# End of a routing stage: the last top two moved ahead of the one-hots, twenty one-hots on GpSimd, and the first low expert weights made before the block ends

## The chip, the cores and the metric

The kernel runs on one core of one Trainium2 chip. A core has five engines that run side by side and meet at semaphores: PE (TensorE, matrix multiply), DVE (VectorE), ACT (ScalarE), POOL (GpSimd) and SP (SyncE, which here only issues DMAs). The metric is the device time in microseconds (us) of one execution, the median over several runs.

## The reference, cut to what matters

Rows `x` of 4 x 1024 tokens with 256 features go through attention with 16 heads, a layer norm, a mixture of experts, and a second layer norm.

```
x = layernorm(x + attention(x))                      # 4096 tokens, 256 features
probs = softmax(x @ gate_W)                          # 8 experts
topk_w, topk_idx = top_k(probs, 2); topk_w /= topk_w.sum(-1)
out = 0.5 * gelu(x @ shared_W + shared_b)
for e in range(8):
    h = gelu(x @ W1[e] + b1[e])                      # 256 -> 1024
    out += combine[:, e] * (h @ W2[e] + b2[e])       # 1024 -> 256
x = layernorm(x + out) * gamma + beta
```

## The kernel before, in words

The program has three stages, each a block of its own: `attention`, `tokens`, `experts` (the second layer norm is the end of the third). A block ends when all five engines have come to its end; only then does the next one begin on any of them.

The change is all in `tokens`, with one line in `experts`. `tokens` goes over 32 tiles of 128 tokens. For each it projects the attention's output (PE, L1052), adds and normalises (DVE, ACT), turns the rows (PE, L1061), multiplies them with the shared and gate weights (PE, L1069), and adds the bias (DVE, L1262). The tiles are routed in four parts: tiles 0 to 7, 8 to 15, 16 to 27 (the third part, `LAST - 1` in the code) and 28 to 31 (the last, `LAST`). For a part there follow:

- `top` (DVE, L1272 to L1285): the two best experts of each token, twelve small instructions each waiting for the one before.
- `rank` (PE, L1077 and L1078; for the last part `last_rank`, L1084 and L1086): how many tokens before this one chose the same expert. For the third part it waits for a running count that POOL makes (L992, L994).
- `places` (DVE, L1293 to L1299): splits a token's place in its expert's list into a high part and a low part of 128.
- `lows`: for each tile and each of the two choices one instruction of 128 x 128 that writes the low part as a one-hot, `low_hot`, 16 bit. Parts one and two have them on POOL (L1002, 16 each), the third on DVE (L1307, 24) and the last on DVE (L1307, 8).

When the last part's counts are there (`totals`, L1096 and L1098), DVE works out where each expert's list begins (L1367 to L1379), and makes the high one-hots in five pieces (`ones_at`, L1313); ACT multiplies each by the row's number (L1202). PE then multiplies low one-hots with high ones (`sort`, L1105, 64 matmuls into one bank): the result says which token stands in each place of the experts' chunks. The five calls of `sort` take choice one of tiles 0 to 15, choice two of tiles 0 to 15, choice one of tiles 16 to 31, choice two of tiles 16 to 23, and choice two of tiles 24 to 31. DVE turns the result into row numbers (L1405 to L1417), POOL gathers the first chunk's rows with two indirect DMAs (L1037), and the block ends. In between DVE makes a small plan of experts (L1384 to L1390); when it is there, SP loads the first expert's weights `up` and `down`.

Matrix products in `experts` are made of three: high times high, low times high, high times low. So each weight is split by ACT into a rounded high part and by DVE into the rest, the low part. The first expert's `up_h` is made by ACT at the end of `tokens` (L1205); its `up_l` by DVE as its first work in `experts` (line L1822, which a helper shares with `e_xl`, the low part of the chunk's turned rows, and `e_w2l`, that of the down weights). PE's first matmuls of `experts` (L1744) need `e_xl`.

Every engine's order is the order in which the code was written; there is no scheduler.

## Time and profile before

| | us |
|---|---|
| median of 3 runs | 1809.6 (1808.56 to 1811.19) |
| the profiled execution | 1826.84 |
| its span, first instruction to last | 1825.1 |
| PE busy | 1730.8 (95%) |
| DVE busy | 1373.6 (75%) |
| ACT busy | 1025.7 (56%) |
| POOL busy | 380.3 (21%) |

The shares are means over the whole program. `attention` ends and `tokens` begins near 1151 us of the span, and `experts` begins at 1338.9 us; the stretch in which the changed code stands is about 1300 to 1342 us, and there no engine is busy all the time. Times in the rows are microseconds from the start of the span unless they are marked ns.

### The profile page before, as it was taken

What the parts mean: (1) busy time and instruction counts of PE and PEld (TensorE: products, weight loads), DVE (VectorE), ACT (ScalarE), POOL (GpSimd) and SP (SyncE); (2) the same over time, 40 slices, a digit from 0 to 9 for tenths busy, and PEclk for the clock granted to TensorE, in tenths of its full rate; (3) what the DMA queues carried; (4) which work ended last, traced back from release to release, by engine and by line L of the source; (5) the groups of instructions that cost most, each with busy time, mean ns of one, the idle gap of its engine ahead of it and who ended that gap; (6) DMA issues with size and microseconds to landing.
All of it is one profiled execution on the core that took longest, in us unless ns stands there. A gap on an engine that the chain in (4) does not pass through costs nothing. (4 is left out here: it accounts for less than half of the span.)

```text
span 1825.1 us, 31876 instructions
## 1 busy us (share of the span) xinstructions
PE 1730.8 (95%) x10919; PEld 1186.5 (65%) x10919; DVE 1373.6 (75%) x2218; ACT 1025.7 (56%) x1529; POOL 380.3 (21%) x422
## 2 busy tenths in 40 slices
PE   6999999999999999999999999799579999999977
PEld 5555555555555555555555554688579999999972
DVE  5888888888888888888888888666656655566647
ACT  5565555655556565565555555466545554555537
POOL 1000000000000000000000000016247666666664
PEclk9999999999999999999999999899889999999998
DMA  5011111111111111311111111465223333233335
GB/s 178 30 35 43 39 37 41 36 36 41 42 36 36 42 41 36 131 36 39 38 41 36 36 41 36 140 216 181 92 77 92 86 89 89 45 87 87 91 59 171
DMA packets 80197, 127.09 MB, mean 70 GB/s; under 512 B 12752, under 2 KB 46736, under 8 KB 77776
## 3 DMA queue, kind: packets, MB, share of 16 engines
q1 hardware_dynamic: 61808, 98.27, 16.3%
q0 software_dynamic: 18272, 27.31, 7.5%
q8 instruction: 67, 1.10, 0.2%
q14 instruction: 50, 0.41, 0.1%
HBM read 86.72 MB, written 38.83 MB: 69 GB/s over the span
## 5 line engine op out<-in xcount | busy, mean ns | idle before, releaser
L447 ACT ACTIVATE a_e<-banks 128x1024 f32<-128x1024 f32 x512 | 483.4, 1033 | 262.3 <-PE banks L344 262.3
L558 DVE TENSOR_TENSOR a_esum<-a_esum,a_e 128x1024 f32<-128x1024 f32 x384 | 470.5, 1225 | 94.6 <-ACT a_e L447 60.8
L358 PE MATMUL banks<-a_e,a_v 128*64 128x512 f32 x2048 | 467.5, 598 | 0.0
L358 PEld LDWEIGHTS banks<-a_e,a_v 128*64 128x64 f32 x2048 | 135.6, 136 | 265.6 <-issue 242.5
L63 POOL MEMSET ident<- 128x128 f32 x1 | 0.2, 205 | 1126.8 <-POOLq L112 1126.8
L344 PE MATMUL banks<-a_qh,a_kh 64*128 64x512 f32 x1024 | 222.2, 428 | 5.7 <-issue 5.3
L344 PE MATMUL banks<-a_qh,a_kl 64*128 64x512 f32 x1024 | 203.9, 390 | 0.0
L344 PE MATMUL banks<-a_ql,a_kh 64*128 64x512 f32 x1024 | 203.9, 392 | 0.0
L1796 ACT ACTIVATE e_g<-banks,e_b1c 128x256 f32<-128x256 f32 x280 | 114.4, 470 | 150.7 <-PE banks L1744 147.3
L344 PEld LDWEIGHTS banks<-a_qh,a_kh 64*128 64x128 f32 x1024 | 97.4, 185 | 144.3 <-issue 97.3
L1757 PE MATMUL banks<-e_w2h,e_hh 128*128 128x256 f32 x560 | 162.3, 290 | 4.9 <-DVE e_hl L1822 2.4
L1744 PE MATMUL banks<-e_xh,up_h 128*128 128x256 f32 x560 | 157.8, 282 | 3.3 <-DVE e_xl L1822 2.0
L1744 PE MATMUL banks<-e_xl,up_h 128*128 128x256 f32 x560 | 157.1, 281 | 1.2 <-issue 1.2
L1744 PE MATMUL banks<-e_xh,up_l 128*128 128x256 f32 x560 | 156.8, 280 | 0.3 <-issue 0.2
L1757 PE MATMUL banks<-e_w2h,e_hl 128*128 128x256 f32 x560 | 156.2, 279 | 0.0
L1757 PE MATMUL banks<-e_w2l,e_hh 128*128 128x256 f32 x560 | 156.2, 279 | 0.0
L1674 POOL DMA_INDIRECT acc_rows<-e_y,e_numbers x70 | 123.7, 1766 | 75.1 <-DVE e_y L1862 59.8
L298 PE MATMUL banks<-a_xh,a_wh 128*128 128x512 f32 x256 | 108.3, 423 | 8.4 <-DVE a_xl L477 8.4
L1757 PEld LDWEIGHTS banks<-e_w2h,e_hh 128*128 128x128 f32 x560 | 105.4, 188 | 11.1 <-DVE e_hl L1822 9.1
L344 PEld LDWEIGHTS banks<-a_qh,a_kl 64*128 64x128 f32 x1024 | 97.7, 186 | 21.3
L1744 PEld LDWEIGHTS banks<-e_xh,up_h 128*128 128x128 f32 x560 | 106.2, 190 | 4.5 <-DVE e_xl L1822 2.4
L456 ACT COPY a_wv<-banks 128x512 f32<-128x512 f32 x64 | 37.5, 587 | 125.2 <-PE banks L358 125.2
(237 smaller groups left out, 3314.0 us busy)
## 6 DMA issues: line engine op xcount, KB each, us to landing
attn_out<-a_ot SPq DMA_DIRECT2D x64, 256.0 KB, 2.0
a_inv<-inv_rows SPq DMA_DIRECT2D x126, 128.0 KB, 2.8
a_w<-w_qkv SPq DMA_DIRECT2D x32, 256.0 KB, 3.1
raw<-attn_out SPq DMA_DIRECT2D x4, 2048.0 KB, 8.9
t_ot<-attn_out SPq DMA_DIRECT2D x4, 2048.0 KB, 9.3
raw<-w_up SPq DMA_DIRECT2D x8, 1024.0 KB
raw<-w_down SPq DMA_DIRECT2D x8, 1024.0 KB
raw<-x_t SPq DMA_DIRECT2D x8, 512.0 KB, 9.4
```

Of the source, the lines that this page charges most:

```text
L63: gpsimd.memset(tile[:, :], 0.0).then_inc(done, 1)
L298: mm = pe.matmul(out[:, :], lhs, rhs, start=m == 0, stop=m == len(parts) - 1)
L344: mm = pe.matmul(tile[:, h * BANK:(h + 1) * BANK], kt[rows, keys], qt[rows, cols], start=part == 0, stop=part == 2)
L358: mm = pe.matmul(o_acc[h * DH:(h + 1) * DH, :], v[quad % 2][:, n, head], e[(slot * ST + n) % NE][:, h * BANK:(h + 1) * BANK], start=n == 0 ...
L447: act.activation(e[t % NE], ring[n % RING], ACT.Exp, scale=SCALE).then_inc(e_ok, 1)
L456: act.copy(o_raw, o_acc).then_inc(o_copied, 1)
L558: dve.tensor_tensor(acc[:, :], acc[:, :], e[(slot * ST + n) % NE], ALU.add).then_inc(add_ok, 1)
L1674: gp.indirect_dma_start(out=acc_rows, in_=y[u][:, a, :], in_offset=None, out_offset=bass.IndirectOffsetOnAxis(ap=numbers_c[u][:, 2, a:a + ...
L1744: mm = pe.matmul(out, lhs, rhs, start=m == 0, stop=m == len(parts) - 1)
L1757: mm = pe.matmul(y_ps[a][:, u * D:(u + 1) * D], lhs[u][:, hb, a * P:(a + 1) * P], rhs[:, wb], start=hb == 0 and m == 0, stop=hb == HB - 1 ...
L1796: act.activation(g[:, hb, :], h_ps[hb // PER][:, (hb % PER) * CHUNK:(hb % PER + 1) * CHUNK], ACT.Gelu, bias=b1c[u][:, hb:hb + 1]).then_inc ...
```

## The change

- `top` for the last part no longer waits behind the third part's low one-hots on DVE. Of these, DVE now makes the twelve of choice one, behind the last `top`; the twelve of choice two go to POOL.
- The last part's eight low one-hots go to POOL as well. On POOL these twenty stand behind the stores of the rows and ahead of the gathers.
- PE now waits for POOL's one-hots in each call of `sort`, with counts of its own (32, 32, 48, 44, 52), where it waited once for 32.
- On PE, `turn` of tiles 30 and 31 now stands ahead of the third part's `rank`.
- DVE makes the first `up_l` at the end of `tokens`, behind the row numbers and a wait for ACT's `up_h`, no longer at the start of `experts`.

The end of DVE's work in `tokens`, from the third part's `places` on. Before (L1299 ends that `places`, L1307 are the low one-hots, L1262 and L1263 the last two tiles' bias and gate values, L1272 the first instruction of the last `top`, L1363 stands behind it, L1293 begins the last `places`):

```order
L1299 SCALAR_TENSOR_TENSOR t_low<-t_high,t_place 128x2x12
L1307 TENSOR_SCALAR t_low_hot<-t_counting,t_low 128x128 x24
L1262 TENSOR_TENSOR t_pre<-banks,raw 128x256
L1263 COPY raw<-banks 128x8
L1262 TENSOR_TENSOR t_pre<-banks,raw 128x256
L1263 COPY raw<-banks 128x8
L1272 TENSOR_REDUCE t_best<-raw 128x4
...
L1285 TENSOR_TENSOR raw<-raw 128x32
L1363 TENSOR_TENSOR r_gap<-t_best 128x32
L1293 TENSOR_TENSOR raw<-banks,raw 128x32 x2
```

The same place of the changed kernel, whose lines are numbered 3 to 4 higher:

```order
L1303 SCALAR_TENSOR_TENSOR t_low<-t_high,t_place 128x2x12
L1266 TENSOR_TENSOR t_pre<-banks,raw 128x256
L1267 COPY raw<-banks 128x8
L1266 TENSOR_TENSOR t_pre<-banks,raw 128x256
L1267 COPY raw<-banks 128x8
L1276 TENSOR_REDUCE t_best<-raw 128x4
...
L1289 TENSOR_TENSOR raw<-raw 128x32
L1366 TENSOR_TENSOR r_gap<-t_best 128x32
L1311 TENSOR_SCALAR t_low_hot<-t_counting,t_low 128x128 x12
L1297 TENSOR_TENSOR raw<-banks,raw 128x32 x2
```

The 24 one-hots ahead of the last top two are gone, and 12 stand between it and the last `places`.

POOL's last work in `tokens` (the stores of `t_shared`, then the gathers), before:

```order
L985 DMA acc_rows<-t_shared 128x4x256
L985 DMA acc_rows<-t_shared 128x2x256 x2
L1037 DMA xg<-x_rows,numbers 128x256 x2
L840 UNCONDITIONAL_BRANCH
```

and in the changed kernel:

```order
L987 DMA acc_rows<-t_shared 128x4x256
L987 DMA acc_rows<-t_shared 128x2x256 x2
L1004 TENSOR_SCALAR t_low_hot<-t_counting,t_low 128x128 x20
L1041 DMA xg<-x_rows,numbers 128x256 x2
L840 UNCONDITIONAL_BRANCH
```

Twenty one-hots now stand between the last store and the two gathers.

DVE at the border of the blocks (L840), before:

```order
L1417 TENSOR_TENSOR numbers<-raw 128x40x2
L840 UNCONDITIONAL_BRANCH
L1819 UNCONDITIONAL_BRANCH
L1822 TENSOR_TENSOR up_l<-raw,up_h 128x2048
L1822 TENSOR_TENSOR e_xl<-banks,e_xh 128x512
```

and in the changed kernel:

```order
L1420 TENSOR_TENSOR numbers<-raw 128x40x2
L1422 TENSOR_TENSOR up_l<-raw,up_h 128x2048
L840 UNCONDITIONAL_BRANCH
L1824 UNCONDITIONAL_BRANCH
L1827 TENSOR_TENSOR e_xl<-banks,e_xh 128x512
```

`up_l` has moved from behind the border to ahead of it.

```diff
--- before.py
+++ after.py
@@ -911,7 +911,9 @@
         last_turned = {t: [n for n in range(TT) if turn_at[n] == t] for t in range(TT + 1)}
         branch_step = {n: EARLY.get(n, turn_at[n + 1] if n + 1 < TT else TT) for n in range(TT)}
         tops = {p: branch_step[part[-1]] for p, part in enumerate(PARTS)}
+        third, last = len(PARTS[LAST - 1]), len(PARTS[LAST])
         early_lows = TOPK * sum(len(part) for part in PARTS[:LAST - 1])
+        lows_for = [early_lows, early_lows, early_lows + third + last, early_lows + third, early_lows + third + TOPK * last]
 
         def tiles(p):
             return slice(PARTS[p][0], PARTS[p][-1] + 1)
@@ -994,10 +996,10 @@
                     link(gp.tensor_tensor(cum[:, t + 1, :], cum[:, t, :], chosen[:, t, :], ALU.add))
                 gp.nop().then_inc(cum_ok, 1)
 
-            def lows(p):
+            def lows(p, choices=range(TOPK)):
 
                 gp.wait_ge(low_ok, p + 1)
-                for j in range(TOPK):
+                for j in choices:
                     for t in PARTS[p]:
                         gp.tensor_scalar(low_hot[:, j, t, :], counting[:, :], low[:, j, t:t + 1], float(MARK + j * TT + t),
                                          ALU.is_equal, ALU.mult).then_inc(lows_ok, 1)
@@ -1031,6 +1033,8 @@
                 while stored < len(GROUPS) and (branch_step[GROUPS[stored][-1]] < t or t == TT):
                     store_shared(stored)
                     stored += 1
+            lows(LAST - 1, range(1, TOPK))
+            lows(LAST)
             gp.wait_ge(rows_out, 16 * len(GROUPS))
             gp.wait_ge(numbers_ok, 1)
             for a in range(CT):
@@ -1101,6 +1105,7 @@
             def sort(part):
                 pe.wait_ge(ones_ok, part + 1)
                 pe.wait_ge(own_ok, part + 1)
+                pe.wait_ge(lows_ok, lows_for[part])
                 for n in range(SORTS[part].start, SORTS[part].stop):
                     mm = pe.matmul(banks[2][:, 0:2 * PT], low_hot[:, n // TT, n % TT, :],
                                    high_hot[:, n, :, :].rearrange("p a b -> p (a b)"), start=n == 0, stop=n == CH - 1)
@@ -1116,10 +1121,10 @@
                 for n in branched_after(t):
                     if turn_at[n] < t:
                         branch(n)
+                for n in turned_after(t):
+                    turn(n)
                 if t == TT:
                     rank(LAST - 1)
-                for n in turned_after(t):
-                    turn(n)
                 for n in branched_after(t):
                     if turn_at[n] == t:
                         branch(n)
@@ -1128,7 +1133,6 @@
                         rank(p)
             last_rank()
             totals()
-            pe.wait_ge(lows_ok, early_lows)
             sort(0)
             sort(1)
             sort(2)
@@ -1302,7 +1306,7 @@
             def lows(p):
 
                 dve.wait_ge(low_ok, p + 1)
-                for j in range(TOPK):
+                for j in range(1):
                     for t in PARTS[p]:
                         dve.tensor_scalar(low_hot[:, j, t, :], counting[:, :], low[:, j, t:t + 1], float(MARK + j * TT + t),
                                           ALU.is_equal, ALU.mult)
@@ -1350,7 +1354,6 @@
                 if t == TT:
                     inverse(ends_group(t - 1))
                     places(LAST - 1)
-                    lows(LAST - 1)
                 for n in branched_after(t):
                     if turn_at[n] == t:
                         biased(n)
@@ -1361,6 +1364,7 @@
                         places(p)
             top(LAST)
             dve.tensor_tensor(gap[:, :], best[:, 1, :], best[:, 0, :], ALU.subtract).then_inc(gap_ok, 1)
+            lows(LAST - 1)
             places(LAST)
 
             dve.wait_ge(totals_ok, 1)
@@ -1389,7 +1393,6 @@
             dve.tensor_copy(plan[:, EXPERT, :], cexp[:, :])
             dve.tensor_tensor(plan[:, NEW, 1:PLANNED], cexp[:, 1:PLANNED], cexp[:, 0:PLANNED - 1], ALU.not_equal)\
                .then_inc(plan_ok, 1)
-            lows(LAST)
             ones_at(2)
             ones_at(3)
             ones_at(4)
@@ -1415,6 +1418,8 @@
             link(dve.scalar_tensor_tensor(beyond[:, :, :], marked, 0.0, spare[:, :, :], ALU.is_equal, ALU.mult))
             dve.tensor_copy(numbers[:, 1:NCHUNK + 1, 1, :], weight_row[:, :, :])
             dve.tensor_tensor(numbers[:, AHEAD:PLANNED, 2, :], target[:, :, :], beyond[:, :, :], ALU.add)
+            dve.wait_ge(up_h_ok, 1)
+            dve.tensor_tensor(up_l[:, :], up[:, :], up_h[:, :].bitcast(F32), ALU.subtract).then_inc(up_l_ok, 1)
 
 
 def outputs(nc, ctx, banks, keep, ident, all_stored, gamma, acc_rows, out):
@@ -1863,8 +1868,6 @@
                                              b2w[:, a, :], ALU.mult, ALU.add).then_inc(y_ok, 1)
 
             prime(dve, y_ok, hl_ok)
-            dve.wait_ge(w1h_ok, 1)
-            low(w1l[:, :], w1[:, :], w1h[:, :], w1l_ok)
             dve.wait_ge(bias_in, 48)
             rows_low(0, 0)
             bias(0, 0)
```

## Rows read from the trace of the kernel before

**Rows 1.** Timeline of DVE: start, us, engine, line, operation, tiles, count [idle before]
```profile
1302.70 4.79 DVE L1307 TENSOR_SCALAR t_low_hot<-t_counting,t_low 128x128 bf16<-128x128 f32 x24
...
1308.34 0.18 DVE L1272 TENSOR_REDUCE t_best<-raw 128x4 f32<-128x32 f32 x1
...
1310.90 0.18 DVE L1363 TENSOR_TENSOR r_gap<-t_best 128x32 f32<-128x32 f32 x1
1313.38 0.29 DVE L1293 TENSOR_TENSOR raw<-banks,raw 128x32 f32<-128x32 f32 x2 [2.29 <-PE banks L1086]
...
1315.52 0.17 DVE L1367 TENSOR_SCALAR r_nch<-banks 128x8 f32<-128x8 f32 x1 [0.78 <-PE banks L1098]
...
1318.63 2.89 DVE L1313 TENSOR_TENSOR r_high_hot<-t_counting,raw 128x1280 bf16<-128x1280 f32 x2
...
1323.00 1.64 DVE L1307 TENSOR_SCALAR t_low_hot<-t_counting,t_low 128x128 bf16<-128x128 f32 x8
1324.57 2.94 DVE L1313 TENSOR_TENSOR r_high_hot<-t_counting,raw 128x1280 bf16<-128x1280 f32 x3
```

**Rows 2.** Timeline of PE
```profile
1301.95 2.05 PE L1069 MATMUL banks<-raw,t_x2t 128*128 128x264 f32 x8 [0.76 <-ACT t_x2t L1166]
1311.04 0.64 PE L1084 MATMUL banks<-raw,t_before 128*128 128x32 f32 x2 [7.04 <-DVE raw L1285]
...
1327.58 1.27 PE L1105 MATMUL banks<-r_high_hot,t_low_hot 128*128 128x160 bf16 x16 [1.49 <-DVE r_high_hot L1313]
...
1328.80 1.27 PE L1105 MATMUL banks<-r_high_hot,t_low_hot 128*128 128x160 bf16 x16
1338.93 1.09 PE L1731 MATMUL banks<-ident,xg 128*128 128x128 f32 x4 [8.87 <-PEq L840]
```

**Rows 3.** Timeline of ACT
```profile
1326.08 2.80 ACT L1202 ACTIVATE r_high_hot<-r_high_hot,t_own 128x1280 bf16<-128x1280 bf16 x3 [3.15 <-DVE r_high_hot L1313]
1328.79 1.90 ACT L1205 CAST up_h<-raw 128x2048 fp32r<-128x2048 f32 x1
...
1340.12 0.58 ACT L1776 CAST e_xh<-banks 128x512 fp32r<-128x512 f32 x1 [9.27 <-PE banks L1731]
```

**Rows 4.** Timeline of POOL, end of the tokens stage
```profile
1308.98 0.72 POOL L985 DMA_DIRECT2D acc_rows<-t_shared  x1 [5.49 <-ACT t_shared L1175]
1333.69 1.04 POOL L1037 DMA_INDIRECT xg<-x_rows,numbers  x1 [23.98 <-DVE numbers L1414]
1335.04 0.96 POOL L1037 DMA_INDIRECT xg<-x_rows,numbers  x1 [0.30 <-issue]
```

**Rows 5.** Timeline of DVE, the row numbers and the border of the blocks
```profile
1332.62 0.20 DVE L1414 CAST numbers<-raw 128x80 uint32<-128x80 f32 x1
...
1333.12 0.23 DVE L1417 TENSOR_TENSOR numbers<-raw 128x80 uint32<-128x80 f32 x1
1339.12 2.29 DVE L1822 TENSOR_TENSOR up_l<-raw,up_h 128x2048 fp32r<-128x2048 f32 x1 [5.76 <-PEq L840]
1341.33 0.68 DVE L1822 TENSOR_TENSOR e_xl<-banks,e_xh 128x512 fp32r<-128x512 f32 x1
```

**Rows 6.** One line's instructions, POOL's low one-hots between 1232 and 1236 us
```profile
L1002 POOL TENSOR_SCALAR t_low_hot<-t_counting,t_low x5: 705/707/735, 1232.7 to 1235.5; 128x128 bf16<-128x128 f32 x5
```

**Rows 7.** Timeline of DVE and POOL, a subtraction beside two low one-hots
```profile
1242.35 1.23 DVE L1221 TENSOR_TENSOR t_otl<-t_ot,t_oth 128x1024 fp32r<-128x1024 f32 x1 [0.52 <-ACT t_oth L1146]
...
1241.64 2.44 POOL L1002 TENSOR_SCALAR t_low_hot<-t_counting,t_low 128x128 bf16<-128x128 f32 x2
```

**Rows 8.** Timeline of POOL and DVE, a store beside DVE's low one-hots
```profile
1302.78 0.71 POOL L985 DMA_DIRECT2D acc_rows<-t_shared  x1 [0.75 <-ACT t_shared L1175]
...
1303.10 0.41 DVE L1307 TENSOR_SCALAR t_low_hot<-t_counting,t_low 128x128 bf16<-128x128 f32 x1
```

**Rows 9.** Timeline of POOL and DVE, indirect DMAs beside a subtraction of 2048
```profile
1344.26 0.94 POOL L1653 DMA_INDIRECT e_wt<-w_rows,e_numbers  x1 [0.30 <-issue]
1345.51 2.07 POOL L1653 DMA_INDIRECT e_wt<-w_rows,e_numbers  x1 [0.30 <-issue]
...
1344.47 2.29 DVE L1822 TENSOR_TENSOR e_w2l<-raw,e_w2h 128x2048 fp32r<-128x2048 f32 x1 [2.33 <-ACT e_w2h L1786]
```

## The prediction

> **What bounds the kernel now.** I read the page first: PE is busy 95% of the span, but the change lies in the one stretch where its share falls, near 1300 to 1342 us. So I went on to the timelines of that stretch, engine by engine, and asked at each idle gap what ended it. The path is one chain. DVE writes the third part's 24 low one-hots from 1302.70 to 1307.49 and only then takes up the last two tiles, whose product PE had at 1304.00 (1301.95 + 2.05) [rows 1, 2]. The last top two runs from 1308.34 to 1311.08; PE, idle for 7.04 us, starts the last rank at 1311.04; DVE waits 2.29 us for it and 0.78 us more for the totals [rows 1, 2]. From 1318.63 come the high one-hots in two batches with the plan and the last part's eight low one-hots between them [rows 1]; ACT follows with 2.80 us for the second batch, and PE's last 33 matmuls run from 1327.58 to 1330.07, when the sort is done [rows 2, 3]. Row numbers are ready at 1332.82 [rows 5], POOL's two gathers end at 1336.00 [rows 4], and PE starts in the experts' block at 1338.93 [rows 2], 2.93 us later. There PE needs `e_xl`, which DVE starts at 1341.33 behind `up_l`, although ACT's part of it is there at 1340.70 [rows 3, 5]. Whatever shortens this chain shortens the kernel, since PE is nearly always busy behind it. Call X the end of the sort (now 1330.07) and N the time of the row numbers (X + 2.75).
>
> **Top two first, step by step.** The last two tiles now take DVE 0.85 us (1307.49 to 1308.34); behind PE's end at 1304.00 only the second is left, some 0.5 us. So top two starts at 1304.5, 3.8 us earlier, and ends at 1307.3. The last rank and the totals hang on it and come 3.8 us earlier too: the last `places` could start at 1309.6 instead of 1313.38.
>
> **Twelve one-hots in the wait.** DVE has 12 left, at 4.79 / 24 = 0.20 us: 2.4 us from 1307.3 to 1309.7. PE's 2.29 us of last rank hide them, if DVE has its usual speed. That cover is what the change lives on. For the last eight one-hots, DVE saves 1.57 us more (1323.00 to 1324.57), so undisturbed the second batch of high one-hots comes 5.4 us earlier.
>
> **Twenty on POOL.** POOL is free when the last store is issued, now 1309.70 [rows 4]; that hangs on the last tile's bias and comes some 3.8 us earlier, at 1305.9. One of its one-hots lasts 0.71 us, and five start between 1232.7 and 1235.5, one each 0.70 us [rows 6]: 14.0 us for 20, against 0.20 us each on DVE. Nor is POOL undisturbed. Beside a DVE subtraction of 1.23 us two of them took 2.44 instead of 1.41 us [rows 7]: POOL stood still for 1.03 of 1.23 us. The five high one-hot instructions are of that kind (two inputs in SBUF), 2.89 and 2.94 us in two batches [rows 1]. They cost POOL some 5.4 us: 1305.9 + 14.0 + 5.4 = 1325.3. Only the last call of `sort` needs the last four; its 8 matmuls take half of 1.27 us, and X would be 1326.1, 4.0 us earlier, with POOL the last to come rather than DVE and ACT (1324.7). PE's new waits cost nothing else: behind them stand only matmuls of the same sort.
>
> **What DVE suffers.** From 1305.9 on POOL's one-hots run beside DVE's twelve and beside the small instructions of the chain, which never happens before. The trace has one near case: a DVE one-hot at 1303.10 took 0.41 us where the 24 need 0.20 us each, and ended at 1303.51, just as a POOL store ended (1302.78 + 0.71) [rows 8]. So POOL can hold back this very instruction. The bounds: 2.4 us for the twelve if POOL never holds them, and 12 x 0.70 = 8.4 us if one gets through per POOL one-hot. No row tells how many get through each time. I take 5.4 us, halfway, which is one or two per POOL one-hot: 3.0 us more. `places` then starts near 1312.7, and by then the totals are there, so the wait of 0.78 us is gone. Eight small `tensor_scalar` and copy instructions of the chain, five of them ahead of the high one-hots, could be held as well; I take 0.2 us each, between 0 and 0.5. Sum up to the second batch: -3.8 + 3.1 (`places` at 1312.7, not 1309.6) - 0.8 + 1.0 + 0.4 - 1.57 = -1.65. X = 1328.4, and POOL, at 12 one-hots by 1315 and the rest by about 1326.5, is not last.
>
> **`up_l` ahead of the border.** The gain: `e_xl` waits for `e_xh` alone, so it starts at about 1340.75 instead of 1341.33, 0.6 us. PE starts that much earlier. The rest of the 2.29 us was hidden by the turn and ACT's copy. The cost is less plain. DVE starts `up_l` when it has finished L1417, at N + 0.5, and runs to N + 2.8. POOL starts the first gather at N + 0.87 (1333.69 against 1332.82), into the middle of it. In the experts' block the same meeting is on record: an indirect DMA that began 0.21 us ahead of a subtraction of 2048 took 0.94 us; the next, begun inside it, took 2.07 us and ended at 1347.58, 0.82 us behind the subtraction's end at 1346.76 [rows 9]. So the first gather would end at N + 3.6, and the second, 0.31 us later and 0.96 us long, at N + 4.9, where it is N + 3.2 now. The border moves with it: +1.7 us. Bounds: 0 if the gather gets in first, 2.3 us if it waits for all of `up_l`. DVE itself is done by then, and `up_h` too: the weights' load is issued behind the plan, and ACT had them by 1328.79 [rows 3], so `up_h` ends well ahead of N + 0.5 in all cases but the slowest.
>
> The Trainium skill has both halves of this in SBUF — State Buffer, section "SBUF: two separate sides": GpSimd and VectorE share a pair of ports that is locked for a whole instruction, by whichever comes first, and the DMAs that GpSimd issues wait too. By that rule, the trace agrees for the indirect DMA (2.07 us) and for POOL's one-hots (2.44 us for two). Against DVE's one-hots it would make each wait for a whole one of POOL's, which is the second rival below; the row at 1303.10 shows one such hold, but behind a store.
>
> **`turn` ahead of `rank`.** ACT copies the turned tiles at about 1301.5, which is later than either order needs; the third part's rank comes 0.1 to 0.3 us later, and so do its places. PE's product at 1304.00 is later still. Between -0.1 and +0.3; I take 0.
>
> **Sum.** -1.65 + 1.7 - 0.6 = -0.55 us, against the profiled execution's 1826.84, so 1826.3. It lies 17.2 us above the median of the runs, nearly all outside this stretch, so I carry the difference over as it is: 1809.6 - 0.5 = **1809.1 us**. A measurement of this kernel can tell 0.2%, 3.6 us, from no change.
>
> **Rivals.**
> 1. POOL and DVE don't get in each other's way on the one-hots. X is 4.0 us earlier; -4.0 + 1.7 - 0.6 = -2.9, 1806.7 us. For it: DVE's subtraction beside POOL's one-hots took 1.23 us in rows 7, no sign of a hold. Against: 0.41 us in rows 8. Chance 0.25.
> 2. Slower: one DVE one-hot per POOL one-hot. The twelve take 8.4 us, `places` starts at 1315.7, 6.1 later than it could; the chain ahead of the second batch is -3.8 + 6.1 - 0.8 + 0.6 + 0.4 - 1.57 = +0.9, and with +1.7 - 0.6 the kernel is 2.0 us slower, 1811.6 us. The side changes when the twelve take more than about 6.0 us, 0.5 us each. For it: the hold in rows 8 lasted until the store's very end. Against: between two POOL one-hots there may be room for more than one of 0.20 us. Chance 0.20.
> 3. The gathers are not held (POOL starts the first before `up_l` gets going, or `up_h` is late). Then -1.65 - 0.6 = -2.2, 1807.4 us, and with rival 1 too, -4.6, 1805.0 us. For it: the start of `up_l` and that of the gather are but 0.4 us apart, and one indirect DMA that was 0.21 us ahead went through. Against: rows 9. Chance 0.15, a third of it with rival 1.
>
> My forecast keeps 0.40. Its own range, with the twelve between 4 and 7 us and the small ones at 0 to 0.5 us, is 1807 to 1811.5. The range for 8 in 10 takes in rivals 1 and 2 with about a microsecond beyond each: 1805.6 to 1812.8. All cases but the double one lie within 3.6 us, yet near enough that their spread crosses it: faster by over 0.2% 0.20, the same 0.64, slower 0.16.
>
> **What would show it.** In the profile of the changed kernel: the last top two starting near 1304.5 and PE's idle of 7.04 us ahead of the last rank cut to 3.2; DVE's twelve at 0.2 us each (rival 1), near 0.45 (forecast) or 0.7 (rival 2); POOL's one-hots stretched beside the high ones; what PE's last sort call waits for, POOL or ACT; the first gather at about 2.7 us instead of 1.04; the border at N + 7.8 instead of N + 6.1; `e_xl` right behind `e_xh`. I am wrong in the mechanism if the twelve take 2.4 us, or if the gathers keep 1.04 and 0.96 us, and in the whole if the median leaves 1805.6 to 1812.8.

## The result

The changed kernel takes 1804.5 us (median of nine runs, 1803.6 to 1805.9); the kernel before, run beside it, 1809.5 us. The ratio is 0.9972, with a 95% interval of 0.9962 to 0.9982: 5.1 us less, where 0.5 us less was predicted and 1805.6 us was the lower end of the range. A second set of runs of the same kernel (below) gave 0.9984 [0.9975, 0.9993], 2.9 us less by the ratio and 3.5 us by the medians; its median of 1805.8 us lies just inside the range. So the gain is real, about 3 to 5 us, and more than the 0.5 us that were forecast in both sets.

The page of the changed kernel shows little: PE is still busy 95% of the span of 1804.1 us. Here are the same places of the timelines as in [rows 1 to 5]. VectorE first:

```profile
1299.43 0.18 DVE L1303 SCALAR_TENSOR_TENSOR t_low<-t_high,t_place 128x24 f32<-128x24 f32 x1
...
1303.32 0.19 DVE L1276 TENSOR_REDUCE t_best<-raw 128x4 f32<-128x32 f32 x1
...
1306.03 0.18 DVE L1366 TENSOR_TENSOR r_gap<-t_best 128x32 f32<-128x32 f32 x1
1306.14 2.83 DVE L1311 TENSOR_SCALAR t_low_hot<-t_counting,t_low 128x128 bf16<-128x128 f32 x12
1308.89 0.28 DVE L1297 TENSOR_TENSOR raw<-banks,raw 128x32 f32<-128x32 f32 x2
...
1309.66 0.30 DVE L1301 TENSOR_SCALAR t_high<-t_high 128x8 f32<-128x8 f32 x1
...
1314.07 2.89 DVE L1317 TENSOR_TENSOR r_high_hot<-t_counting,raw 128x1280 bf16<-128x1280 f32 x2
...
1318.59 2.94 DVE L1317 TENSOR_TENSOR r_high_hot<-t_counting,raw 128x1280 bf16<-128x1280 f32 x3
...
1328.30 2.28 DVE L1422 TENSOR_TENSOR up_l<-raw,up_h 128x2048 fp32r<-128x2048 f32 x1
1337.65 0.69 DVE L1827 TENSOR_TENSOR e_xl<-banks,e_xh 128x512 fp32r<-128x512 f32 x1 [7.06 <-ACT e_xh L1781]
```

The twelve one-hots took 2.83 us, 0.236 us each. The prediction had them at 5.4. The `places` behind them no longer waits for PE. The high one-hots' second batch starts 19.0 us behind the end of the third part's places (1299.61), 21.9 us in the kernel before (1302.67 to 1324.57). Now PE, whose last rank had waited 7.04 us [rows 2]:

```profile
1298.86 3.89 PE L1073 MATMUL banks<-raw,t_x2t 128*128 128x264 f32 x8 [1.13 <-ACT t_x2t L1170]
1306.17 0.64 PE L1088 MATMUL banks<-raw,t_before 128*128 128x32 f32 x2 [3.42 <-DVE raw L1289]
...
1317.06 5.99 PE L1110 MATMUL banks<-r_high_hot,t_low_hot 128*128 128x160 bf16 x48 [6.45 <-DVE r_high_hot L1317]
...
1324.38 0.71 PE L1110 MATMUL banks<-r_high_hot,t_low_hot 128*128 128x160 bf16 x8 [0.67 <-POOL t_low_hot L1004]
1335.77 1.08 PE L1736 MATMUL banks<-ident,xg 128*128 128x128 f32 x4 [10.68 <-PEq L840]
```

In this execution the last branch took 3.89 us, not 2.05, and held the top two back; the sort ends at 1325.10. Its last call waits for GpSimd, which worked without a gap to 1324.24, and whose first gather now takes 2.83 us:

```profile
1303.96 0.72 POOL L987 DMA_DIRECT2D acc_rows<-t_shared  x1 [3.56 <-ACT t_shared L1179]
1304.78 19.46 POOL L1004 TENSOR_SCALAR t_low_hot<-t_counting,t_low 128x128 bf16<-128x128 f32 x20
1328.71 2.83 POOL L1041 DMA_INDIRECT xg<-x_rows,numbers  x1 [4.47 <-DVE numbers L1417]
1331.85 0.97 POOL L1041 DMA_INDIRECT xg<-x_rows,numbers  x1 [0.30 <-issue]
```

### The profile page after: what moved, and what is told of

Same layout as the page of the kernel before. It is cut to its first block and busy times, and to the rows that moved or that the text cites. A ratio compares the mean times of both kernels' runs of the same rounds, so it can differ in the third digit from the quotient of the medians.

```text
span 1804.1 us, 31876 instructions
## 1 busy us (share of the span) xinstructions
PE 1722.6 (95%) x10919; PEld 1182.8 (66%) x10919; DVE 1371.4 (76%) x2198; ACT 1027.3 (57%) x1529; POOL 398.5 (22%) x442
## 5 line engine op out<-in xcount | busy, mean ns | idle before, releaser
L358 PE MATMUL banks<-a_e,a_v 128*64 128x512 f32 x2048 | 467.5, 598 | 0.0
L1679 POOL DMA_INDIRECT acc_rows<-e_y,e_numbers x70 | 120.0, 1714 | 60.1 <-DVE e_y L1867 40.5
L1849 DVE CAST e_hh<-e_g 128x512 fp32r<-128x512 f32 x140 | 60.0, 428 | 66.6 <-ACT e_g L1801 66.0
```

The lines of the kernel that those rows point to most:

```text
L358: mm = pe.matmul(o_acc[h * DH:(h + 1) * DH, :], v[quad % 2][:, n, head], e[(slot * ST + n) % NE][:, h * BANK:(h + 1) * BANK], start=n == 0 ...
L1679: gp.indirect_dma_start(out=acc_rows, in_=y[u][:, a, :], in_offset=None, out_offset=bass.IndirectOffsetOnAxis(ap=numbers_c[u][:, 2, a:a + ...
L1849: dve.tensor_copy(hh[u][:, these, :], g[:, these, :]).then_inc(hh_ok, 1)
```

## The experiments

In the tables, X' is the end of the sort (X) less the end of the third part's places, which takes out when the stage began. "PE" is the start of the first up matmul of the experts' block on the same scale. The branch column is the last branch's duration and stands for PE's clock at that moment. All columns from X' on come from one profiled execution of each kernel, and the first two rows are the two kernels' own first profiles. The sets were timed at different times, some of them on different chips, each with the kernel before beside it; the ratio is to that one.

| kernel | median us | ratio [interval] | X' us | N to border | PE us | branch us |
|---|---|---|---|---|---|---|
| before | 1809.5 | | 27.40 | 6.11 | 39.40 | 2.05 |
| change | 1804.5 | 0.9972 [0.9962, 0.9982] | 25.49 | 7.92 | 38.78 | 3.89 |
| null | 1808.3 | 0.9998 [0.9989, 1.0007] | 28.80 | 6.12 | 40.81 | 3.89 |
| up_only | 1810.4 | 1.0005 [0.9996, 1.0014] | 28.92 | 7.86 | 42.16 | 2.79 |
| up_home | 1805.5 | 0.9977 [0.9967, 0.9986] | 23.65 | 6.08 | 35.63 | 2.05 |
| up_late | 1804.9 | 0.9972 [0.9963, 0.9981] | 23.66 | 6.20 | 35.25 | 2.05 |
| again | 1805.8 | 0.9984 [0.9975, 0.9993] | 23.63 | 7.94 | 36.96 | 2.05 |
| last_only | 1810.3 | 1.0004 [0.9995, 1.0013] | 26.88 | 7.86 | 40.13 | 2.05 |
| all_dve | 1809.5 | 0.9996 [0.9987, 1.0005] | 26.34 | 7.87 | 39.59 | 2.05 |
| last_dve | 1806.4 | 0.9986 [0.9978, 0.9995] | 24.00 | 7.94 | 37.32 | 2.05 |
| up_twice | 1805.9 | 0.9981 [0.9972, 0.9990] | 23.63 | 8.85 | 37.86 | 2.05 |
| four_back | 1802.0 | 0.9956 [0.9944, 0.9969] | 23.03 | 6.18 | 34.59 | 2.05 |
| warm_before | 1810.6 | 1.0002 [0.9993, 1.0011] | 28.98 | 6.08 | 40.94 | 2.86 |
| warm_best | 1804.2 | 0.9970 [0.9958, 0.9982] | 22.60 | 6.15 | 34.13 | 2.05 |

An interval of 0.0009 is 1.6 us to either side. Terms of one or two microseconds are therefore read from the profiles. There the terms of VectorE, ScalarE and GpSimd repeat within 0.1 us; those of PE do only where its clock is the same, as null and again will show. The medians serve as a check on the sum.

**null: the kernel before, again.**

> The kernel before, word for word, profiled and timed once more. It tells what the profiled execution of before, 17 us above the median of its runs, held that the runs did not, and how far two equal kernels differ. Both theories: ratio 1.000 within 0.001. If the profile's excess belongs to that one execution, this one's experts block, from PE's first L1744 to its last, is some 15 us shorter than the first profile's; if it belongs to the kernel, it is as long as there.

The ratio is 0.9998. The profile is worth more: its span is 1806.2 us, and from PE's first up matmul to the end it needs 465.5 us where the first profile of before had 483.0. So the 17 us by which that profile exceeded its runs belong to that one execution. X' is 28.80, though, 1.4 us more than in that profile. PE's last calls show why:

```profile
1324.84 2.29 PE L1105 MATMUL banks<-r_high_hot,t_low_hot 128*128 128x160 bf16 x16 [1.49 <-DVE r_high_hot L1313]
...
1327.14 1.52 PE L1105 MATMUL banks<-r_high_hot,t_low_hot 128*128 128x160 bf16 x16
```

The first sixteen of these took 1.27 us in [rows 2]. The granted clock stood at 0.5 (1.2 GHz) here until 1327.7, and there had risen by 1326.7, ahead of the call. The instructions are the same.

**The up weights' low part: up_only, up_home, up_late, up_twice.** The first makes this move alone in the kernel before; the second takes it back out of the change:

```
# up_only: before, with these two lines at the end of the tokens stage
+            dve.wait_ge(up_h_ok, 1)
+            dve.tensor_tensor(up_l[:, :], up[:, :], up_h[:, :].bitcast(F32), ALU.subtract).then_inc(up_l_ok, 1)
...
-            low(w1l[:, :], w1[:, :], w1h[:, :], w1l_ok)
# up_home: the change, with the same lines the other way round
```

> Before with up_l moved to the end of the tokens block and nothing else. Theory: 1.7 us for the held gather less 0.6 us for e_xl: 1.1 us slower than before, 1810.6 us. Rival (the gain is in the move): 2 us or more faster than before.

> The change with up_l moved back to the start of the experts block. Theory: the first gather is held by up_l, 1.7 us, and e_xl gains 0.6 us, so without the move the kernel is 1.1 us faster than the change, near 1803.4 us; its first gather lasts 1.04 us and not 2.83. Rival: the move is what the change gains by, because up_l no longer holds POOL's copy and gathers at the start of experts; then this one falls back towards before, to 1807 us or more.

up_late keeps it in the tokens stage, behind both gathers:

```
+            gp.memset(told[:, :], 0.0).then_inc(gathered, 1)      # GpSimd, behind the gathers
...
+            dve.wait_ge(gathered, 1)
             dve.wait_ge(up_h_ok, 1)
```

> The change with up_l still in the tokens block but behind the two gathers: POOL sets one element behind the second gather, and DVE waits for it. Theory: the gathers keep 1.04 and 0.96 us, up_l runs while the border is crossed and ends before it, e_xl keeps its gain: 1.7 us faster than the change, near 1802.8 us. Rival (the hold costs nothing that counts): as the change, 1804.5 us within 0.5.

up_twice computes it twice ahead of the border:

```
+            link(dve.tensor_tensor(up_l[:, :], up[:, :], up_h[:, :].bitcast(F32), ALU.subtract))
             dve.tensor_tensor(up_l[:, :], up[:, :], up_h[:, :].bitcast(F32), ALU.subtract).then_inc(up_l_ok, 1)
```

> The change with the low part of the up weights computed twice in a row ahead of the gathers. Theory (the first gather waits for the subtraction on VectorE, and PE waits for the gathers at the border): the first gather ends 0.8 us behind the second subtraction, the border comes 2.3 us later than in the change (10.2 us behind the row numbers), 1806.8 us, ratio 0.9985. Rival (a delay of the border is absorbed by the first chunks of the experts, where the weights' arrival or PE's clock bounds the time): border 2.3 us later, but the first chunks' starts are not, and the time is 1804.5, ratio 0.9972. Third: the gather is started ahead of the second subtraction and held once only: the border moves by less than 1 us.

All profiles agree on the hold. The first gather takes 2.8 us wherever the subtraction is ahead of it (up_only, change, again) and 1.1 us in up_home and up_late; the border comes 7.9 us behind the row numbers in the former and 6.1 to 6.2 us in the latter. up_twice shows the hold once per subtraction, VectorE first, then GpSimd:

```profile
1328.37 2.29 DVE L1422 TENSOR_TENSOR up_l<-raw,up_h 128x2048 fp32r<-128x2048 f32 x1
1330.69 2.29 DVE L1423 TENSOR_TENSOR up_l<-raw,up_h 128x2048 fp32r<-128x2048 f32 x1
```

```profile
1328.78 2.83 POOL L1041 DMA_INDIRECT xg<-x_rows,numbers  x1 [4.48 <-DVE numbers L1417]
1331.92 1.90 POOL L1041 DMA_INDIRECT xg<-x_rows,numbers  x1 [0.31 <-issue]
```

The first gather ends 0.95 us behind the first subtraction, inside the second one; the second gather, begun inside the second subtraction, ends 0.84 us behind it. The border moves by 0.9 us and not 2.3: the third of the expectations holds, in which a gather is held by the subtraction that it meets at its start and by no later one. The other half of the move, PE starting 2.62 instead of 3.13 us behind the border, is in every kernel with the subtraction ahead of the experts. Net, up_only should cost 1.2 us; its ratio of 1.0005 is 0.9, with an interval that takes in no change at all. Between change, up_home and up_late the medians show no order: 1804.5 and 1805.8, 1805.5, 1804.9. Their profiles differ by 1.3 and 1.7 us up to PE's start, but the time from that start to the end of the kernel was 465.7, 466.4, 467.4 and 467.5 us in them, so the remainder of one execution scatters by as much. Both versions were expected to be faster than the change (1803.4 and 1802.8 us) and neither was. So it is not shown that the 1.7 us reach the end. The recorded rival of up_late, that the hold costs nothing that counts, fits its 1804.9 us as well, and up_home's other rival, a fall back to 1807 us or more, did not come about.

**Which part of the sort's gain is whose: all_dve, last_dve, last_only.** These give the one-hots back to VectorE. all_dve has all 24 of the third part behind the last top two and the last eight where they were:

```
-            lows(LAST - 1, range(1, TOPK))     # GpSimd
-            lows(LAST)
...
-                for j in range(1):             # VectorE
+                for j in range(TOPK):
...
+            lows(LAST)
             ones_at(2)
```

> The change with none of the last two parts' low one-hots on GpSimd: VectorE makes all 24 of the third part behind the last top two (12 more than the change), and the last part's eight ahead of the fourth and fifth calls' high one-hots, as before. Theory (what the change gained is VectorE time behind the last top two; the one-hots cost what they cost alone, 0.20 us each): places of the last part +2.0 us over the change (24 in 4.8 us where twelve took 2.83), the eight +1.6, PE's wait of 0.67 us for GpSimd gone: end of the sort 2.9 us later relative to the third part's places, 1807.4 us, ratio to before 0.9988. Rival (the gain comes from the top two's earlier place and PE's order alone, and the one-hots on VectorE lie beside PE's last ranks): 1804.5, ratio 0.9972.

last_dve gives back only the eight:

```
             lows(LAST - 1, range(1, TOPK))     # GpSimd
-            lows(LAST)
...
+            lows(LAST)                         # VectorE
             ones_at(2)
```

> The change with the last part's eight low one-hots on VectorE, where they were before; GpSimd keeps the third part's twelve. Theory: VectorE 1.57 us longer ahead of the last calls' high one-hots, PE no longer waits 0.67 us for GpSimd's last one: end of the sort +0.9, 1805.4 us, ratio 0.9977. Rival (GpSimd's eight beside the high one-hots hold VectorE as much as they save it): the sort ends 0.7 us earlier than in the change, 1803.8, ratio 0.9968; then each high one-hot and small operation of this stretch is shorter than in the change.

last_only moves only the eight, with the 24 on VectorE ahead of the top two:

```
-            lows(LAST - 1, range(1, TOPK))     # GpSimd; its lows(LAST) stays
...
                     places(LAST - 1)
+                    lows(LAST - 1)             # VectorE, all 24
...
-            lows(LAST - 1)
             places(LAST)
```

> The change with the third part's 24 low one-hots on VectorE where they were before, ahead of the last top two; GpSimd makes the last part's eight only. Theory (each part of the change is worth the VectorE time that it takes off the chain): only the 1.6 us of the last eight are gained, GpSimd needs 5.7 us for eight plus what the high one-hots hold it and is done before ScalarE's part; the sort ends 26 to 27.2 us behind the third part's places (27.4 or 28.8 before), the gathers cost 1.3 net: 1809.1 us, ratio 0.9998. Rival (GpSimd, started only when the last places are there, ends behind ScalarE's high one-hots): PE's last call waits for it, the sort ends beyond 27.5, 1810 or more, ratio 1.0003.

Undisturbed, 24 one-hots behind the top two take VectorE as long as they did ahead of it; the twelve of last_dve, with GpSimd at work beside them, are the change's:

```profile
1306.64 4.79 DVE L1309 TENSOR_SCALAR t_low_hot<-t_counting,t_low 128x128 bf16<-128x128 f32 x24
```

```profile
1304.42 2.84 DVE L1310 TENSOR_SCALAR t_low_hot<-t_counting,t_low 128x128 bf16<-128x128 f32 x12
```

So GpSimd costs the twelve 0.4 us, against 2.4 us for half of 24. The second batch of high one-hots starts 19.59 us behind the third part's places in all_dve, 18.55 in last_dve and 17.14 in the change with a fast branch (again, below). Of the 2.45 us of all_dve, 1.95 are the twelve more, -0.12 a top two that ends earlier, -0.81 the small instructions that GpSimd no longer holds, and 1.42 the eight; of last_dve's 1.41 all are the eight. The sort of all_dve ends 2.7 us later, where 2.9 was expected. That this comes so near is partly luck. In both versions PE waits for the second batch and then has 32 matmuls left; all_dve ran the first sixteen of them at the lower clock, last_dve at the higher one:

```profile
1324.63 2.29 PE L1108 MATMUL banks<-r_high_hot,t_low_hot 128*128 128x160 bf16 x16 [1.49 <-DVE r_high_hot L1315]
```

```profile
1322.46 1.27 PE L1109 MATMUL banks<-r_high_hot,t_low_hot 128*128 128x160 bf16 x16
```

From the start of the second batch to the end of the sort last_dve needs 5.45 us and all_dve 6.75. With last_dve's 5.45 us all_dve would end only 1.4 us behind the change, an estimate from these two profiles. X' is 24.00 in last_dve and 23.63 in the change, so here the eight on GpSimd bring 0.37 us, not 1.5; with the last calls at the lower clock they would bring some 1.3 us more. The expectation for last_dve was 0.9 us later. The medians, 1806.4 beside 1804.5 and 1805.8, agree in sign, but last_dve's own runs reach from 1804.4 to 1811.3. In last_only GpSimd begins its eight only when the last places are there:

```profile
1313.77 8.31 POOL L1004 TENSOR_SCALAR t_low_hot<-t_counting,t_low 128x128 bf16<-128x128 f32 x8 [5.14 <-DVE t_low L1302]
```

Eight times 0.70 us is 5.6; the other 2.7 us are the hold by one batch of high one-hots. Still it ends at 1322.08, well ahead of ScalarE, and X' is 26.88, within the expectation. The kernel is no faster than before (1.0004). With the gathers held, moving the eight alone shows no gain, and neither does the earlier top two with all one-hots still on VectorE (all_dve, 0.9996). The earlier top two with the third part's twelve on GpSimd, and without the eight, does (last_dve, 0.9986). So what carries the change is the top two's earlier place with half the one-hots gone from VectorE's path. All three versions keep `turn` ahead of `rank`, which no run takes back.

**again: the change once more.**

> The change once more. In its first profile PE had its lower clock at the last branch (3.89 us where before had 2.05), so the last top two ended 6.4 us behind the third part's places instead of the 4.6 of five kernels built on it. Theory (the clock at that moment differs from execution to execution and is no part of the change): the sort ends 23.7 us behind the third part's places, or 25.5 with the slow branch; 1804.5 us, ratio 0.9972. Rival (the change itself causes the slow branch): 25.5 again, with 3.89 us for the branch.

The branch is back at 2.05 us and X' at 23.63; PE waits only 0.28 us for GpSimd:

```profile
1299.97 2.05 PE L1073 MATMUL banks<-raw,t_x2t 128*128 128x264 f32 x8 [1.13 <-ACT t_x2t L1170]
1305.43 0.63 PE L1088 MATMUL banks<-raw,t_before 128*128 128x32 f32 x2 [3.42 <-DVE raw L1289]
...
1323.63 0.71 PE L1110 MATMUL banks<-r_high_hot,t_low_hot 128*128 128x160 bf16 x8 [0.28 <-POOL t_low_hot L1004]
```

So the change does not cause the slow branch; null, without the change, had it too. Whether the change makes it rarer is open. Of the ten profiles with `turn` ahead of `rank`, nine have the branch at the higher clock; of the four with the old order (before, null, up_only, warm_before), one has. The new order puts `turn` into PE's wait ahead of the third part's rank: PE is idle there for 1.5 us in again, 2.1 us in before. In the change a slow branch costs 1.8 us of X', 25.49 against 23.63; in before VectorE's 24 one-hots cover it.

**warm_before, warm_best: PE kept busy ahead of the sort.** Both add, behind the totals,

```
+            for _ in range(14):
+                pe.matmul(banks[1][:, 0:4 * P], low_hot[:, 0, 0, :], low_hot[:, 0, 0:4, :].rearrange("p a b -> p (a b)"),
+                          start=True, stop=True)
```

> The kernel before, with 14 matmuls of 512 columns into an unused bank while PE waits for the first high one-hots; their result is not read. Theory (before's sort ends 1.4 us later in two profiles of three, 28.8 instead of 27.4 us behind the third part's places, because PE has its lower clock in the last calls: 2.29 us for 16 matmuls instead of 1.27): with PE busy ahead of the sort the clock is up, the 16 matmuls behind the second batch take 1.27 us, the sort ends at 27.2 to 27.4; 1808.4 us, ratio 0.9994. Rival (the matmuls do not change when the clock rises, or the sort's end follows something else): 28.8, ratio 1.0000.

> The version with the up weights' low part behind the gathers and four one-hots back on VectorE, with 14 matmuls of 512 columns into an unused bank while PE waits for the first high one-hots; their result is not read. There PE's first three calls of the sort (5.98 us for 46 matmuls on record) end after ScalarE's last high one-hots, so PE sets the end. Theory (a fast PE takes itself off the path): the calls end before ScalarE does, and the sort ends 1.2 us behind ScalarE, 22.6 instead of 23.0 us behind the third part's places: 1801.5 us, ratio 0.9954. Rival (the clock falls again within the sort, or the extra matmuls hold the first call): 23.0 or more, 1802 or more, ratio 0.9956 or above.

The rows of warm_before:

```profile
1314.37 5.36 PE L1133 MATMUL banks<-t_low_hot 128*128 128x512 bf16 x13 [0.23 <-issue]
1320.32 2.67 PE L1105 MATMUL banks<-r_high_hot,t_low_hot 128*128 128x160 bf16 x32 [0.59 <-DVE r_high_hot L1316]
1326.24 2.29 PE L1105 MATMUL banks<-r_high_hot,t_low_hot 128*128 128x160 bf16 x16 [3.25 <-DVE r_high_hot L1316]
```

```profile
core 0: us, PE busy (x) PEld busy (x) DVE busy (x) ACT busy (x) POOL busy (x), PEclk, DMA share, GB/s
1314.00:1320.00 6.00, 5.50 (x14) 1.91 (x15) 5.49 (x12) 1.18 (x1) 0.00 (x0) 0.57 0.00 0
1320.00:1326.00 6.00, 2.53 (x32) 2.19 (x32) 5.90 (x18) 2.81 (x3) 0.00 (x0) 1.00 0.39 134
1326.00:1331.00 5.00, 4.01 (x33) 3.77 (x33) 1.57 (x8) 3.48 (x5) 0.00 (x0) 0.66 0.64 265
```

The clock did rise early: 32 matmuls took 2.67 us instead of 4.43. But then PE waited 3.25 us for the second batch, the clock fell again at 1326.0, and the last calls were slow after all. X' is 28.98 and the theory's gain is absent. It fails in one half: the filler changes when the clock rises, and does not keep it up where the path needs it. In warm_best X' is the 22.60 expected, but the median, 1804.2, is no better than four_back's. That kernel's profile has PE start 0.46 us earlier than four_back's, and its median is 2.2 us higher, so the medians of these small sets don't order such versions. No gain of the fillers is shown.

**four_back: the best version that the runs point to.** It puts the up weights' low part behind the gathers, as up_late, and the last part's four second-choice one-hots where VectorE would otherwise wait for PE:

```
-            lows(LAST)                          # GpSimd
+            lows(LAST, range(1))
...
             dve.tensor_tensor(w_all[:, TT:CH], e2[:, :], w1[:, :], ALU.mult).then_inc(w_all_ok, 1)
+            for t in PARTS[LAST]:               # VectorE
+                dve.tensor_scalar(low_hot[:, 1, t, :], counting[:, :], low[:, 1, t:t + 1], float(MARK + TT + t),
+                                  ALU.is_equal, ALU.mult).then_inc(four_ok, 1)
```

> The change with two edits: the up weights' low part behind the gathers, and the last part's four low one-hots of the second choice on VectorE, behind the weights of all tokens. Theory: GpSimd ends its one-hots about 3 us earlier and PE's last call no longer waits for it (-0.7 us; the four cost VectorE 0.8 us where it otherwise waits for PE's sums), the gathers are not held (-1.7): 1802.1 us, ratio 0.9959. Rival (the border's 1.7 us are absorbed, and the four on VectorE cost the 0.8 us that PE gains): 1804.5, ratio 0.9972.

GpSimd, then VectorE, then PE of this kernel:

```profile
1305.18 14.07 POOL L1005 TENSOR_SCALAR t_low_hot<-t_counting,t_low 128x128 bf16<-128x128 f32 x16
1328.50 1.08 POOL L1042 DMA_INDIRECT xg<-x_rows,numbers  x1 [9.24 <-DVE numbers L1424]
```

```profile
1322.64 0.87 DVE L1409 TENSOR_SCALAR t_low_hot<-t_counting,t_low 128x128 bf16<-128x128 f32 x4
1324.92 0.24 DVE L1415 TENSOR_SCALAR raw<-banks 128x80 f32<-128x80 f32 x1 [1.41 <-PE banks L1114]
```

```profile
1323.61 1.27 PE L1114 MATMUL banks<-r_high_hot,t_low_hot 128*128 128x160 bf16 x16
1333.82 1.08 PE L1744 MATMUL banks<-ident,xg 128*128 128x128 f32 x4 [8.93 <-PEq L840]
```

PE's last call no longer waits for GpSimd, and the four lie in a wait of VectorE of which 1.41 us are left. X' is 0.6 us less than the change's, the border 1.7 us nearer to the row numbers. The kernel takes 1802.0 us against an expectation of 1802.1; its interval lies wholly below that of again and overlaps that of the change's first set, so against the change it is faster by 2.5 to 3.9 us in the medians, and clearly so against one set of two. The profiles give 2.4 us up to PE's start (34.59 against again's 36.96). With five runs, and with 1804.2 us for the same version with fillers, that the time came out as expected is weak support. It beats the kernel before by 0.44% [0.31, 0.56].

## Why the prediction was wrong

**The step that failed** is "Twelve one-hots in the wait" with "What DVE suffers": 5.4 us for the twelve, halfway between bounds of 2.4 and 8.4. They took 2.83. The chain up to the second batch shows the share of each term, with again (fast branch) against the first profile of before:

| term of the chain | predicted | measured |
|---|---|---|
| last top two earlier | -3.8 | -3.65 (its end 8.24, now 4.59 us behind the places) |
| top two to the last `places` | +3.1 | +0.4 (2.48 us before, 2.86 now) |
| `places` to high one-hots, with the totals' wait | +0.2 | -0.1 (5.25, now 5.18) |
| first to second batch | -1.17 | -1.4 (5.94, now 4.52) |
| sum | -1.65 | -4.8 |

Of the 3.1 us that are missing, 2.7 are the twelve. The bounds were right and the choice between them was not. The halfway value had no row behind it, and [rows 8] was misread. It set a duration, 0.41 us, against a step from start to start, 0.20 us. One such one-hot lasts 0.28 us and overlaps the next. The one at 1303.10 was 0.13 us longer in its record, and the next started 0.20 us behind it as always, so the series lost nothing: 24 take 4.79 us with that store beside them [rows 1] and 4.79 us in all_dve with no GpSimd instruction beside them. Nor was it so that GpSimd's one-hots had never run beside VectorE's small instructions. The trace of before has a `tensor_scalar` with one input in SBUF inside GpSimd's first sixteen:

```profile
1240.94 0.20 DVE L1248 TENSOR_SCALAR t_var<-t_mv 128x4 f32<-128x4 f32 x1
```

```profile
1232.68 14.17 POOL L1002 TENSOR_SCALAR t_low_hot<-t_counting,t_low 128x128 bf16<-128x128 f32 x16 [5.84 <-DVE t_low L1299]
```

It took 0.202 us, and 0.205 us at 1276.36 inside the second sixteen; its seven calls with GpSimd's one-hots away took 0.17. That is 0.03 us of hold and pointed to the lower bound. [Rows 7], named under rival 1, pointed the same way, with a subtraction. The profile of the change says it in single instructions: while one GpSimd one-hot ran, 1307.66 to 1308.49, VectorE started its own at 1307.85, 1308.07, 1308.27 and 1308.47. Of the eleven steps from one of the twelve to the next, nine are 0.20 to 0.23 us, one is 0.40 and one 0.30.

This step alone does not bring the forecast to the first set's result. With 2.8 us for the twelve the prediction becomes its own rival 1, and 1806.7 us is still 2.2 us above the 1804.5 measured (see the sum below).

**The end of the sort.** GpSimd was predicted at 14.0 + 5.4 = 19.4 us for its twenty, and took 19.46. That it would be the last to come was said for the case in which VectorE is not held ("Twenty on POOL", rival 1), which is what happened: PE's last call waits for it, and of VectorE's 4.8 us X keeps 3.8 (27.40 to 23.63). The prediction's own forecast had it in time, which followed from the wrong 5.4 us alone.

**The small instructions.** Held as predicted, but less. Between the last `places` and the high one-hots all_dve, with GpSimd idle, needs 4.37 us and the change 5.18; with some 0.15 us of wait for the totals in it, the holds are about 0.7 us there, where 1.0 was taken. L1301 took 0.30 us instead of 0.17. Between the batches it is 4.52 less 4.37, 0.15 where 0.4 was taken. (The recorded sum has a slip here: eight instructions at 0.2 us are 1.6, of which it carries 1.4, and rival 2 takes 0.6 for the five without saying why. Neither changes the outcome.)

**`up_l` ahead of the border.** Right: the first gather ends at N + 3.7 (predicted 3.6), the second at N + 4.97 (4.9), the border comes at N + 7.92 (7.8), and `e_xl` starts right behind `e_xh`, which brings 0.51 us (0.6). **`turn` ahead of `rank`**, taken as nothing, is nothing for the places: the third part's end 7.41 us behind PE's last projection matmul in the first profile of before and 7.44 in the change's. What it does to PE's clock at the last branch, the prediction did not ask; the counts under again leave that open, and it wasn't tried by itself.

**The sum.** Put together from measured terms, -3.8 + 1.8 - 0.5 = -2.5 us, rival 1's -2.9 within half a microsecond. It had a chance of 0.25, and its time, 1806.7, was inside the range. The second set, -2.9 us, is near that; the first, -5.1, is 2.6 us more. Part of the rest is in the frame of reference. X' was 27.40 in the profile that the prediction was made from, but 28.80, 28.92 and 28.98 in the other three kernels with the old order of the sort, whose last calls met the lower clock. Against those the sort ends 5.2 us earlier, and the sum is -3.9 us. The profiles hint at a reason why the new order should be spared: wherever the second batch is there in time, PE goes from the second call into the third with no wait, and the clock rose within that call or ahead of it (1.3 to 2.0 us for its sixteen matmuls in eight profiles). Where PE waits about 1.5 us or more between them, the sixteen took 2.29 us in four profiles and 1.27 in two. How often each happens in the runs that were timed, no profile tells. The test by warm_before didn't settle it, as it could not hold the clock up. So the 2.7 us of the twelve are shown; that PE's clock at the last calls makes up the rest is likely and open. In its favour, the two sets' intervals share the stretch from 0.9975 to 0.9982, 3.3 to 4.5 us less, which holds -3.9 and not -2.5. That is weak: the two sets of one and the same kernel differ by 1.3 us in their medians, and null by 1.0 us from the kernel before beside it.

**The range** took in rivals 1 and 2 with a microsecond beyond, and the double case (rivals 1 and 3), 1805.0, lay outside. It had no allowance for the profile of before being on one side of what differs between executions.

The Trainium skill says in SBUF — State Buffer, section "SBUF: two separate sides", that between a GpSimd instruction and a VectorE one that runs in a two-port mode or reads two tensors in SBUF, the pair of ports goes to whichever starts first for its whole instruction. The prediction left that condition on the VectorE instruction out when it drew its second rival from the rule. The gathers and GpSimd's one-hots against VectorE's subtractions and high one-hots bear out that the loser waits for a whole instruction (2.83 us; 19.46 us for 14.0). That the first to start wins they do not: the subtraction at 1242.35 [rows 7] started 0.02 us behind the second GpSimd one-hot (1242.33) and took its usual 1.23 us, and the one-hot took 1.75. VectorE's low one-hots read one tensor in SBUF. No hold of a whole GpSimd instruction (0.70 us) appears among the twelve, and their mean is 0.236 us. Which mode they ran in, no row shows.

## What to carry to other kernels

Where a shared resource has bounds far apart, look through the whole trace for a row with the very pair of operations, compare durations with durations and steps with steps, and price each direction by itself: here GpSimd waits for VectorE's instructions of two SBUF operands, and hardly the reverse. An operation issued just behind the start of a long subtraction on VectorE is held to the subtraction's end, so put the subtraction behind the transfers that the next stage waits for. And take a second profile of the kernel before, if there is one, before reading a term of a microsecond from it: the same matmuls took 1.27 or 2.29 us by when the clock rose.

## What the runs showed of the hardware

- A GpSimd one-hot that meets VectorE's high one-hots lasts 3.17 to 3.31 us instead of 0.70: it is held for a whole batch (2.89 or 2.94 us) and does not get in between the batch's two or three instructions. Each batch costs GpSimd about 2.7 us (19.46 us less 20 times 0.70, by two). The other way round little is lost: VectorE's twelve low one-hots took 2.83 us beside GpSimd's, 2.4 without.
- An indirect DMA is held by the subtraction that runs when it starts, not by one that starts later (up_twice: the first gather was done 0.92 us into the second subtraction).
- PE's granted clock changes at moments that differ from execution to execution by several us against the same instructions: the last branch took 2.05, 2.79, 2.86 or 3.89 us. The Trainium skill says in TensorE: Matmul & The Clock Gate, section "Part 1: The HAM clock gate", that the phase runs free of the kernel and the number of slow matmuls varies from run to run; the trace agrees (before and null are the same program, with 2.05 and 3.89 us), and here it sits on the critical path.
- Filling PE's wait raised the clock (granted share 1.0, 2.4 GHz) for the 32 matmuls behind it (4.43 to 2.67 us), and behind PE's next wait, of 3.25 us, the last calls ran at the lower clock (0.5, 1.2 GHz) again. (The trace has 13 of the 14 fillers.)
